# Loading the first rows of signs in three portions, and making the first pair's taps and weights by themselves

## The reference

```python
x = x + depthwise(gn(x), taps0)     # layer 0: taps made from the data
x = x + conv3x3(sign(gn(x)), sign(W))   # layer 1: dense, signs only
x = x + depthwise(gn(x), taps2)     # layer 2
x = x + depthwise(gn(x), taps3)     # layer 3

def gn(v):      # groups of 2 channels: (v - mean) / sqrt(var + 1e-5)
def taps(v):    # v is gn(x)
    hidden = relu(v.mean(axis=(2, 3)) @ w1 + b1)      # 128 wide
    return (hidden @ w2 + b2).reshape(b, 32, 3, 3)    # one 3 x 3 kernel per image and channel
```

## Time and profile before

| | |
|---|---|
| median of 3 runs | 4350.15 us (4338.25 to 4359.49) |
| the profiled execution's own time | 4354.15 us |
| its span, first to last instruction | 4352.3 us |
| PE busy | 3142.5 us, 72% |
| DVE, ACT, POOL busy | 48%, 41%, 45% |
| mean granted clock of TensorE | 0.873 of full speed |

### The profile page before, as it was taken

The page is one execution under the profiler, slowest core; times in us unless marked ns, Lnnn a source line. Parts: engine busy times, 40 slices in busy tenths (PEclk is TensorE's granted clock), DMA queues, the critical chain, the costliest instruction groups (busy, mean ns, idle before and its releaser), DMA issues.

```text
span 4352.3 us, 69714 instructions
## 1 busy us (share of the span) xinstructions
PE 3142.5 (72%) x26176; PEld 2008.6 (46%) x26176; DVE 2069.2 (48%) x6038; ACT 1786.4 (41%) x2626; POOL 1957.0 (45%) x3175
## 2 busy tenths in 40 slices
PE   0675987758876588865887667867778759777598
PEld 0443645435454354633545434554445535445355
DVE  2626643266432764327543275333844257432573
ACT  2433633335333463434534354333543436324232
POOL 1326544264432653336533464425643265431754
PEclk9987998879988798987998879888889889888799
DMA  6288697876969769596694967969678697786946
GB/s 210 57 147 168 151 318 200 155 164 140 340 175 170 159 159 322 159 195 153 182 330 119 212 148 197 306 118 216 149 217 292 109 212 165 234 270 111 200 76 218
DMA packets 589270, 829.46 MB, mean 191 GB/s; under 512 B 489731, under 2 KB 490502, under 8 KB 572550
## 3 DMA queue, kind: packets, MB, share of 16 engines
q1 hardware_dynamic: 323200, 734.28, 66.5%
q10 hardware_dynamic: 216582, 76.68, 8.2%
q0 software_dynamic: 49152, 14.05, 2.0%
HBM read 375.89 MB, written 267.45 MB: 148 GB/s over the span
## 4 chain that ended last, share of the span: by engine, by line
PE 46%; DMA 21%; DVE 9%; SPq 8%; ACT 5%; POOL 4%; ACTq 3%; issue 3%; DVEq 0%; POOLq 0%
PE acc L961 26%; PE acc L978 14%; SPq L327 6%; DMA dense_out<-arena 5%; DMA out<-y 4%; DMA arena<-x 4%; POOL y L510 4%; PE acc L1040 3%; DMA arena<-signs 3%; DVE dense_stats L860 2%; DMA signs<-arena 2%; DMA arena<-y 2%; ACT arena L599 2%; ACTq L535 2%; ACTq L606 2%
## 5 line engine op out<-in xcount | busy, mean ns | idle before, releaser
L961 PE MATMUL acc<-y,arena 64*128 64x384 f32 x9216 | 1749.3, 508 | 190.1 <-ACT y L568 129.0
L961 PEld LDWEIGHTS acc<-y,arena 64*128 64x128 f32 x9216 | 1013.6, 197 | 777.4 <-ACT y L568 229.2
L327 POOL DMA_DIRECT2D arena<-y x1536 | 790.6, 522 | 837.3 <-PE acc L978 736.4
L568 ACT ACTIVATE y<-acc 128x768 f32<-128x768 f32 x832 | 645.1, 807 | 1177.5 <-PE acc L978 1176.6
L978 PE MATMUL acc<-arena 64*128 64x384 f32 x4608 | 953.9, 509 | 195.2 <-issue 195.2
L489 POOL TENSOR_SCALAR arena<-arena,cst,fill 128x24 f32<-128x24 f32 (+1 forms) x1536 | 614.3, 419 | 701.8 <-issue 450.4
L510 POOL TENSOR_TENSOR y<-arena,y 128x3072 f32<-128x3072 f16 x88 | 529.8, 6043 | 734.5 <-DMA arena<-dense_out 734.3
L860 DVE BATCH_NORM_STATS2 dense_stats<-y 128x6 f32<-128x192 f32 x1536 | 408.0, 345 | 728.4 <-POOL y L510 728.2
L978 PEld LDWEIGHTS acc<-arena 64*128 64x128 f32 x4608 | 518.1, 196 | 422.3 <-issue 228.2
L1040 PE MATMUL acc<-arena,wd_side 128*32 128x384 fp8e4 (+1 forms) x10752 | 470.4, 329 | 290.3 <-DMA arena<-signs 231.5
L802 DVE TENSOR_SCALAR_CACHE_REDUCE y<-acc 128x768 f32<-128x768 f32 x256 | 245.1, 958 | 624.3 <-PE acc L978 624.3
(11 more groups left out here) (84 smaller groups left out, 1145.6 us busy)
## 6 DMA issues: line engine op xcount, KB each, us to landing
y<-x SPq DMA_DIRECT2D x64, 2304.0 KB, 26.1
out<-y SPq DMA_DIRECT2D x64, 2304.0 KB, 23.6
arena<-y SPq DMA_DIRECT2D x768, 141.0 KB
arena<-x SPq DMA_DIRECT2D x168, 576.0 KB, 6.4
dense_out<-arena ACTq DMA_DIRECT2D x384, 192.0 KB, 6.9
arena<-dense_out SPq DMA_DIRECT2D x192, 384.0 KB, 6.8
arena<-y SPq DMA_DIRECT2D x768, 71.9 KB
arena<-signs SPq DMA_DIRECT2D x192, 250.0 KB, 10.4
```

Source lines behind the costliest of these rows:

```text
L327: eng.dma_start(halo[at:at + n, slot, :, d0:d0 + size], y[source:source + (n - 1) * step + 1:step, first + odd:first + odd + 3:2, s0:s0 + ...
L568: nc.scalar.activation(y[:, 2 * g:2 * g + 2, k * KN:(k + 1) * KN], acc[:, 2 * k:2 * k + 2, 0:KN], ACT.Identity, accum_out=sums[:, g, k:k + ...
L961: nc.tensor.matmul(acc[:, 2 * k + odd, 0:KN], w_center[at, slot, 2 * q + odd, :], y[at, 2 * g + odd, k * KN:(k + 1) * KN], start=turn == 0 ...
```

## The change

The loads of the dense layer's first window are cut into three portions by channel. The first (channels 0 to 23) is issued once pair 13 of layer 0 is finished and batches 0 to 5 are written. Then batch 6 is written, waited for and loaded, and then batch 7. Other windows are loaded as before. So that the first window may be filled while layer 0 still works, its place in the arena moves from byte 0 to behind the staging of the results, where a halo slot and a weights slot that are no longer used lie.

On the other side, `tap_products` makes the 18 taps of pair 0 by themselves ahead of all 288, and DVE's order at the start of a layer becomes: taps and weights of pair 0; halo taps and weights of batch 0; taps and weights of pair 1; taps of the other 28 channels; halo taps of the other 14 pairs. Several small results in PSUM move to other banks, and PE's product for the variances waits for `fill` in layer 0 alone.

```diff
-A_SIGN = 0
-A_DSTAGE = A_SIGN + 2 * SIGN_BYTES
-A_D = A_DSTAGE + SUBS * WN * 2
+A_DSTAGE = SIGN_BYTES
+A_SIGN = [A_DSTAGE + SUBS * WN * 2, 0]
+A_D = A_SIGN[0] + SIGN_BYTES
...
-        ps_gmean = acc[:, 6, 0:C]
...
+        ps_gmean = [acc[:, k, o:o + C] for k, o in ((7, FREE), (5, 0), (5, 0))]
+        ps_half = [acc[:, k, o:o + C] for k, o in ((7, FREE + C), (5, C), (5, C))]
+        ps_var = [acc[:, k, o:o + C] for k, o in ((7, FREE + 2 * C), (4, 0), (4, 0))]
...
-            def load_signs(s, w):
+            def load_signs(s, w, first, last):
...
-                            sign_in[w % 2][q:q + 32, 0:SUBS * PLANE].rearrange("p (u n) -> p u n", u=SUBS),
-                            signs[p2:p2 + 63:2, :, w * WROWS * PITCH:w * WROWS * PITCH + PLANE]
+                            sign_in[w % 2][q + first:q + last, 0:SUBS * PLANE].rearrange("p (u n) -> p u n", u=SUBS),
+                            signs[p2:p2 + 63:2, first:last, w * WROWS * PITCH:w * WROWS * PITCH + PLANE]
...
+            def wait_signs_written(s, batches):
+
+                for k in range(2):
+                    sp.wait_ge(sign_out[k], 16 * 2 * (BATCHES // 2 * s + (batches + 1 - k) // 2))
+
+            def first_signs(s):
+
+                ahead_ch = (BATCHES - 2) * BATCH_CH
+                sp.wait_ge(acc_full[THIRDS - 1], 2 * (s * ND * PAIRS + (BATCHES - 1) * BATCH_PAIRS))
+                wait_signs_written(s, BATCHES - 2)
+                load_signs(s, 0, 0, ahead_ch)
+                for b in range(BATCHES - 2, BATCHES):
+                    write_signs(s, b)
+                    wait_signs_written(s, b + 1)
+                    load_signs(s, 0, b * BATCH_CH, (b + 1) * BATCH_CH)
...
-                    if b > 0:
+                    if 0 < b < BATCHES - 1:
                         write_signs(s, b - 1)
-                write_signs(s, BATCHES - 1)
-                sp.wait_ge(acc_full[THIRDS - 1], 2 * (s * ND + 1) * PAIRS)
-                for k in range(2):
-                    sp.wait_ge(sign_out[k], 16 * 2 * (BATCHES // 2) * (s + 1))
-                load_signs(s, 0)
-                load_signs(s, 1)
+                first_signs(s)
+                load_signs(s, 1, 0, C)
...
+            def pair_centers(d, g):
+
+                if d > 0:
+                    dve.wait_ge(acc_full[THIRDS - 1], 2 * (d * BATCHES - 1) * BATCH_PAIRS)
+                at = slice(2 * g, 2 * g + 2)
+                by_row("c", turned_c[:, at], spread_c[:, at], 2)
+                by_column("c", spread_c[:, at], w_center[:, 0, at], 2).then_inc(center_ready, 1)
...
+            def first_weights(d):
+
+                dve.wait_ge(first_taps_ready, d + 1)
+                turn_centers(slice(0, 2), ps_first.rearrange("p (c t) -> p c t", t=TAPS))
+                pair_centers(d, 0)
+                dve.wait_ge(taps_ready, d + 1)
+                turn_halos(slice(0, BATCH_PAIRS))
                 halo_weights(0)
-                turn_centers(slice(BATCH_CH, C))
+                turn_centers(slice(2, BATCH_CH), by_tap[:, 2:BATCH_CH])
+                pair_centers(d, 1)
+                turn_centers(slice(BATCH_CH, C), by_tap[:, BATCH_CH:C])
+                turn_halos(slice(BATCH_PAIRS, PAIRS))
...
             def group_variances(d):
                 pe.wait_ge(spread_ready, d + 1)
-                pe.wait_ge(fill_ready, d + 1)
+                if d % ND == 0:
+                    pe.wait_ge(fill_ready, d + 1)
...
             def tap_products(d):
                 li = d % ND
-                nc.tensor.matmul(ps_taps, cst[:, C_SEL + li * P:C_SEL + (li + 1) * P], b2_sb[:], start=True, stop=False)
-                pe.wait_ge(hidden_ready, d + 1)
+                sel = cst[:, C_SEL + li * P:C_SEL + (li + 1) * P]
+                if li == 0:
+                    pe.wait_ge(hidden_ready, d + 1)
+                nc.tensor.matmul(ps_first, sel, b2_sb[:, 0:2 * TAPS], start=True, stop=False)
+                nc.tensor.matmul(ps_taps, sel, b2_sb[:], start=True, stop=False)
+                if li > 0:
+                    pe.wait_ge(hidden_ready, d + 1)
+                nc.tensor.matmul(ps_first, hidden[:], w2_sb[:, li, 0:2 * TAPS], start=False, stop=True)\
+                    .then_inc(first_taps_ready, 1)
                 nc.tensor.matmul(ps_taps, hidden[:], w2_sb[:, li, :], start=False, stop=True).then_inc(taps_ready, 1)
```

More of the change, by code:

```diff
@@ L249, in conv_preact_kernel @@
                  .rearrange("p (c g w) -> p c g w", c=BATCH_CH, w=PITCH) for k in range(2)]
-        sign_in = [part(A_SIGN + k * SIGN_BYTES, SIGN_BYTES, F8) for k in range(2)]
+        sign_in = [part(A_SIGN[k], SIGN_BYTES, F8) for k in range(2)]
         d_stage = part(A_DSTAGE, SUBS * WN * 2, F16).rearrange("p (u n) -> p u n", u=SUBS)
@@ L289, in conv_preact_kernel @@
         hidden_ready = sem("hidden_ready")
+        first_taps_ready = sem("first_taps_ready")
         taps_ready = sem("taps_ready")
@@ L659, in _ @@
                 .then_inc(masks_ready, 1)
-            nc.vector.memset(acc[:, 7, :], 0.0)
+            nc.vector.memset(spread_all, 0.0)
             dve.wait_ge(dense_in, 16 * 4)
@@ L701, in by_column, with center_weights @@
                     mask[of][2].rearrange("p (a b) -> p a b", a=4).unsqueeze(1).to_broadcast([P, n, 4, 4 * R]), ALU.mult)
-            def center_weights(d, chunk, parts=1):
-                slot = chunk % W_CHUNKS
+            def center_weights(d, chunk):
                 before = (d * BATCHES + chunk - W_CHUNKS + 1) * BATCH_PAIRS
@@ L709, in center_weights @@
                 by_row("c", turned_c[:, chunk * BATCH_CH:(chunk + 1) * BATCH_CH], spread_c, BATCH_CH)
[L710 to L713, removed]
+                by_column("c", spread_c, w_center[:, chunk % W_CHUNKS], BATCH_CH).then_inc(center_ready, BATCH_PAIRS)
+            def pair_centers(d, g):
[4 more added lines that the diff above has]
+                by_column("c", spread_c[:, at], w_center[:, 0, at], 2).then_inc(center_ready, 1)
             def halo_weights(chunk):
@@ L764, in hidden_layer, with turn_centers @@
                                         ALU.add, ALU.max).then_inc(hidden_ready, 1)
-            def turn_centers(chans):
+            def turn_centers(chans, product):
                 n = chans.stop - chans.start
-                link(nc.vector.tensor_tensor(taps[:, chans], by_tap[:, chans],
+                link(nc.vector.tensor_tensor(taps[:, chans], product,
                                              rstd[:, chans].unsqueeze(2).to_broadcast([P, n, TAPS]), ALU.mult))
@@ L772, in turn_centers, with turn_halos @@
                 turn("c", taps[:, chans], turned_c[:, chans], n)
[L774 to L779, removed]
+            def turn_halos(pairs):
+                n, ends = pairs.stop - pairs.start, slice(2 * pairs.start, 2 * pairs.stop)
                 for odd in range(2):
@@ L782, in first_halos @@
                     ins = nc.vector.tensor_tensor(
-                        halo_taps[at], by_tap[at, odd:C:2, :],
-                        rstd[at, odd:C:2].unsqueeze(2).to_broadcast([HALF, PAIRS, TAPS]), ALU.mult)
+                        halo_taps[at, pairs], by_tap[at, ends.start + odd:ends.stop:2, :],
+                        rstd[at, ends.start + odd:ends.stop:2].unsqueeze(2).to_broadcast([HALF, n, TAPS]), ALU.mult)
                 link(ins)
-                link(nc.vector.tensor_reduce(tap_sum[:], halo_taps[:], AX.X, ALU.add))
-                link(nc.vector.scalar_tensor_tensor(tap_sum[:], tap_sum[:], -1.0, gmean[:, 0:C:2], ALU.mult, ALU.mult))
+                link(nc.vector.tensor_reduce(tap_sum[:, pairs], halo_taps[:, pairs], AX.X, ALU.add))
+                link(nc.vector.scalar_tensor_tensor(tap_sum[:, pairs], tap_sum[:, pairs], -1.0,
+                                                    gmean[:, ends.start:ends.stop:2], ALU.mult, ALU.mult))
                 link(nc.vector.copy_predicated(
-                    halo_taps[:], shift_mask.unsqueeze(2).to_broadcast([P, PAIRS, TAPS]),
-                    tap_sum[:].unsqueeze(2).to_broadcast([P, PAIRS, TAPS])))
-                turn("h", halo_taps[:], turned_h, PAIRS)
+                    halo_taps[:, pairs], shift_mask.unsqueeze(2).to_broadcast([P, n, TAPS]),
+                    tap_sum[:, pairs].unsqueeze(2).to_broadcast([P, n, TAPS])))
+                turn("h", halo_taps[:, pairs], turned_h[:, pairs], n)
+            def first_weights(d):
[4 more added lines that the diff above has]
+                turn_halos(slice(0, BATCH_PAIRS))
                 halo_weights(0)
-                turn_centers(slice(BATCH_CH, C))
+                turn_centers(slice(2, BATCH_CH), by_tap[:, 2:BATCH_CH])
+                pair_centers(d, 1)
+                turn_centers(slice(BATCH_CH, C), by_tap[:, BATCH_CH:C])
+                turn_halos(slice(BATCH_PAIRS, PAIRS))
             def evict(d, g):
@@ L826, in depthwise @@
                     hidden_layer(d)
-                    first_centers(d)
-                    first_halos()
+                    first_weights(d)
```

(16 more changed lines are left out.)

29 lines of the change are left out of this document (14 added, 15 removed).

## The result

The changed kernel takes 4409.33 us (median of 4 runs, 4392.54 to 4420.42) against 4352.44 us for the kernel before (4 runs). The ratio is 1.0129, with a 95% interval of 1.01 to 1.0157. The forecast was 4349 and the range ended at 4373. The profiled execution has a span of 4418.6 us, 66.3 more than before.

A forecast was written before the change was run, and what follows sets the result against it. The prediction held that no one engine bounds the kernel. Its terms, 8 x (-1.9 - 1.7 + 3.0) + 4 = -1 us against the profiled 4354.15, gave 4353, about 4349 us as a median; range 4297 to 4373.

The forecast's parts named there:

- part 1: Sign loads ahead of the dense layer: cutting the first window into three portions gains 1.9 us an image.
- part 3: DVE's longer chain at layer starts: hidden in layer 1, +3.0 us an image in layer 2, +4 us once at d = 0.
- a transfer with 4 partitions runs on a quarter of the engines: Sign loads, portions of 4 channels: 512 pieces run as 128 on each of four engines, 5.0 us at 39 ns.
- T: End of layer 0's last sign instruction (L584) in an image; PE's dense start was at T+16.0 before.
- T+4.1+2x: Predicted start of PE's dense layer with three portions: T+14.1 with x = 5.0, a gain of 1.9 us.
- x: Transfer time of a four-channel portion of signs: taken as 5 us, with ends at 1.3 and 12 us.
- break-even at x = 6 us: Sign loads: the portion time x from which the three portions no longer gain.
- T-to-PE: Time from the last sign to the first dense product: 16.0 us before, 14 forecast, 24 or more by rival (b).
- rival (b): Sign loads: four target partitions are slower still, x = 10 to 12; 64 to 95 us lost, 4413 to 4444; chance 0.12.
- the second window follows ... hidden: Dense layer's second sign window: arrives some 10 us of transfer after the first, beside PE's work, at no cost.
- Part 2: Start of layers 1 and 2 up to PE's pair 0: PE begins 1.7 us earlier (0.6, 0.8, 0.2, rounded up).
- Rival (c): Layer 2: DVE's longer chain costs nothing more while layer 1 gains; 1 to 3 us an image better, 4325 to 4340; chance 0.12.

The follow-up runs named there:

- `weights_only`: The kernel before with the first pair's taps and weights change alone, sign loads as before: 4379.59 us, ratio 1.0075.
- `weights_act_evicts`: `weights_only` with ACT instead of DVE evicting third 0 of pair 0 in layer 2: 4329.18 us, ratio 0.9933 against the kernel before.

## Why the prediction was wrong

**The direction** was missed, and with it the range. Two terms did it: of the some 58 us between the forecast's -1 and the measured +57, part 1 makes 8 x (1.9 + 3.2) = 41 us, and part 3 about 10.

**The failed step of part 1** is "a transfer with 4 partitions runs on a quarter of the engines, so 512 pieces are 128 on each of four, 5.0 us at 39 ns". I divided the rate by engines. The runs show a rate that goes with how many groups of neighbouring target partitions a transfer covers and not with its engines: 59 GB/s and 109 at about the same share of the engines (1.50 and 1.44). The portion takes 8.0 us alone and 10.3 (12.1 less 1.8) with the second window behind it. So the 39 ns a piece and engine were not the engine's own time, and the share of 1.44 that I read as saturation does not show it. The rest of the working held roughly: batch 7's write landed at T+7.8 against T+6.9, and T+4.1+2x gives x = 7.5 from the 19.2 us measured. The break-even at x = 6 us is the same sum and was not measured by itself. The term was put at -1.9 us an image and measured +3.2, or +2.8 alone (T-to-PE 18.8 against 16.0). This is the mechanism of rival (b), at 40% of its smaller price. The third portion's x was 8 to 10 us and not 10 to 12, and the second portion was issued at T-3.4 (796.28) and not T-2.2, which took back a part. That the measured 4409 lies next to (b)'s 4413 is luck: that figure left out parts 2 and 3, and with them it would be 8 x (8.0 - 1.7 + 3.0) + 4 = 78 us more than before, about 4428.

The line "the second window follows ... hidden" was off too: it shares the third portion's way, 1.4 us an image (17.4 against 18.8).

**Part 2 was right.** -1.7 us a start; measured -1.5 (layer 1) and -1.6 to -1.7 (layer 2).

**Part 3 had the right mechanism, and its sum was a little small.** DVE's chain 14.7 us, measured 14.2; PE's wait 5.2, measured 4.8; pair 1's products at 5.2 us, measured 5.6 on the mean of eight images (4.1 before), so the lower clock costs 1.4 and not 1.1. Layer 2 was put at +3.0 us over the old end. In `weights_only` it is (45.5 - 6.8) / 7 = 5.5 us from pair 0's start, less 1.6, that is +3.9. Of the 5.5, the longer wait makes 3.2 and the slower products 1.8 (5.9 us on the mean in this kernel against 4.1); the remaining 0.5 is open, and no more than the scatter, since kernels with layer 2 unchanged sum to 2065 to 2083 us in this stretch. At d = 0 it was +6.8 and not +4. Rival (c) fell: `weights_act_evicts` shows that the wait itself was the price.

By the forecast's own sum with what was measured: 8 x (+3.2 - 1.5 + 3.9) + 7 = 52 us against 57 between the medians.

Why a group of four partitions is a limit, the runs don't show. The Trainium skill ("DMA: Bandwidth & Descriptors", section on the descriptor swizzle) places each four neighbouring partitions on one port into SBUF, partitions 32 to 63 on the same ports as 0 to 31, and 64 to 127 on others. What was measured is in line with it: 16 spread partitions at the rate of 32, and the gain from having targets below and above 64 in work at once. That it is the port was not tested by itself, and a limit of pairs of partitions, of the DRAM side or of a single queue is not ruled out by these runs.

## What to carry to other kernels

When a load is cut to start it early, cut it so that the piece left on the path is shorter in time, not in bytes: a strip of a few neighbouring target partitions may take as long as the whole, however full the engines look. Compare two windows with the same engine share and different widths before pricing it. When a chain of small instructions is reordered so that its first result comes sooner, look at what stands behind the whole chain in the same queue; here moving one eviction of 1 us to another engine, ACT, turned a loss of 0.75% into a gain of 0.67%.

## What the hardware showed that was not expected

DMA pieces of 250 bytes from DRAM went at 13.6 to 15 GB/s for each group of four neighbouring target partitions, whether 1, 4, 6 or 8 groups were in the transfer. Two queues whose targets lie below and above partition 64 moved 187 GB/s where one moved 110; which of the two, the queues or the targets, does it was not separated. TensorE's granted clock was 0.50 after PE had stood still for 6.3 us, and waits of 3.8 to 5.8 us put pair 1's 20 products at 4.9 to 6.5 us in all eight images instead of 3.50 us (granted clock 0.53 to 0.71 on the mean). In the kernel before, these products took 3.50 us behind the five waits of 0.7 to 1.8 us (granted clock 1.00), and 5.19 us behind the three of 2.1 to 2.2 us (0.67 on the mean).
